# Output product of the linear attention layer as three products of split parts, with x2 held one group at a time

## The reference

```
x = _layernorm(x)                                   # of the outer step
h = _layernorm(x, ln1_g, ln1_b)
Q = phi(h @ Wq); K = phi(h @ Wk); V = h @ Wv        # 16 heads of 64, phi = elu + 1
num_t = Q_t @ sum_{s<=t} K_s V_s^T;  den_t = Q_t . sum_{s<=t} K_s
x = x + (num / max(den, 1e-6)) @ Wo                 # the product that is changed
x = x + gelu(_layernorm(x, ln2_g, ln2_b) @ Wf1) @ Wf2
```

## Time and profile before

| | |
|---|---|
| median of three runs | 4540.95 us |
| the three runs | 4534.86, 4540.95, 4541.82 us |
| the profiled execution, its own time | 4534.58 us |
| its span | 4532.8 us |
| TensorE busy | 4069.8 us, 90% |
| VectorE busy | 2799.5 us, 62% |
| ScalarE busy | 1909.9 us, 42% |
| GpSimd busy | 1185.3 us, 26% |
| HBM traffic | 38 GB/s over the span |
| mean granted TensorE clock | 0.95 |

### The profile page before, as it was taken

How to read it: one execution, slowest core, us unless ns; L and a number is a source line. 1 busy time by engine, 2 the same in 40 slices (tenths; PEclk the granted TensorE clock), 3 DMA queues, 4 the chain that set the end, 5 groups by cost and what they waited for, 6 DMA issues and landing times. The chain is left out here.

```text
span 4532.8 us, 78162 instructions
## 1 busy us (share of the span) xinstructions
PE 4069.8 (90%) x26868; PEld 3109.3 (69%) x26868; DVE 2799.5 (62%) x8170; ACT 1909.9 (42%) x3047; POOL 1185.3 (26%) x1096
## 2 busy tenths in 40 slices
PE   4999999999994899999999999999999599999992
PEld 2344444444442688888888888888888498989892
DVE  4787887887871655565656655555665465555555
ACT  1566665666663333332333433333433233333333
POOL 3233343433422311111111111111111133333334
PEclk8899999999996999999999999999999699999996
DMA  3443443453321100000000000000000133333335
GB/s 70 87 91 62 81 98 54 76 113 59 57 67 58 36 14 16 20 19 11 18 15 16 14 12 16 16 4 14 14 13 27 41 64 61 64 62 64 60 74 205
DMA packets 169072, 222.84 MB, mean 49 GB/s; under 512 B 27148, under 2 KB 144235, under 8 KB 168672
## 3 DMA queue, kind: packets, MB, share of 16 engines
q1 hardware_dynamic: 140640, 181.14, 17.1%
q0 software_dynamic: 25728, 28.03, 4.0%
q10 hardware_dynamic: 2304, 8.39, 0.5%
HBM read 85.92 MB, written 87.05 MB: 38 GB/s over the span
## 5 line engine op out<-in xcount | busy, mean ns | idle before, releaser
L812 ACT ACTIVATE probs<-a_scores 128x1024 f32<-128x1024 f32 (+3 forms) x768 | 614.8, 811 | 367.4 <-PE a_scores L716 361.6
L973 DVE CUSTOM_DVE_ANT_0 a_scores<-a_scores,mask 128x384 f32<-128x384 f32 (+3 forms) x1024 | 482.1, 515 | 117.8 <-PE a_scores L702 112.1
L716 PEld LDWEIGHTS a_scores<-q_st,k_st 50*128 50x128 f32 x1536 | 149.6, 192 | 405.7 <-issue 273.4
L269 POOL TENSOR_TENSOR l_ln_rstd<-l_ln_ve,minus_half 128x4 f32<-128x4 f32 x80 | 84.0, 1050 | 1196.9 <-DVE l_ln_ve L242 1196.7
L716 PE MATMUL a_scores<-q_st,k_st 50*128 50x512 f32 (+3 forms) x1536 | 350.9, 455 | 32.7 <-issue 24.8
L976 DVE TENSOR_REDUCE mx<-a_scores 128x2 f32<-128x1024 f32 x256 | 310.5, 1223 | 109.5 <-PE a_scores L702 108.3
L702 PE MATMUL a_scores<-k_st,q_st 48*128 48x512 f32 (+3 forms) x1536 | 307.1, 398 | 47.6 <-ACT probs L812 29.9
L736 PE MATMUL a_out<-probs,v_aug 128*32 128x512 f32 (+3 forms) x3072 | 347.7, 526 | 1.9 <-POOL probs L905 1.8
L905 POOL TENSOR_SCALAR_AFFINE_SELECT probs<-probs 128x512 f32<-128x512 f32 x256 | 162.7, 636 | 558.7 <-ACT probs L812 555.3
L2333 PE MATMUL e_out<-e_weights_lo,e_hT_hi 128*128 128x256 f32 x1088 | 308.1, 283 | 0.0
L2333 PE MATMUL e_out<-e_weights_hi,e_hT_lo 128*128 128x256 f32 x1088 | 307.6, 283 | 0.0
(11 more groups left out here) (259 smaller groups left out, 10195.4 us busy)
## 6 DMA issues: line engine op xcount, KB each, us to landing
q_st<-parts SPq DMA_DIRECT2D x192, 128.0 KB, 4.4
k_st<-parts SPq DMA_DIRECT2D x192, 128.0 KB, 6.0
expert_rows_scratch<-empty_row SPq DMA_DIRECT2D x34, 520.0 KB, 8.7
e_weights<-in_L_ffn_W_dram SPq DMA_DIRECT2D x16, 1024.0 KB, 6.8
e_rows<-expert_rows_scratch SPq DMA_DIRECT2D x24, 390.0 KB
e_rows<-expert_rows_scratch SPq DMA_DIRECT2D x16, 520.0 KB
x_in<-in_L_attn_x_dram SPq DMA_DIRECT2D x8, 1024.0 KB, 5.7
expert_sums_scratch<-empty_row SPq DMA_DIRECT2D x8, 1024.0 KB, 12.0
```

Of the source, the lines that this page charges most:

```text
L716: last = nc.tensor.matmul(psum_r[:, R.slot(u), h2, 0:w], k_st[rows, 2 * hg + pair, i * P:(i + 1) * P], q_st[rows, 2 * hg + pair, q0:q0 + w ...
L812: nc.scalar.activation(probs[:, k % 3, 2 * pair:2 * pair + 2, 0:w], psum_r[:, R.slot(u), :, 0:w], ACT.Exp).then_inc(R.evacuated[R.slot(u)], 1)
L973: last = nc.vector.tensor_tensor_reduce(s, s, mask[:, HALF - w:HALF], 1.0, LEAST, ALU.add, ALU.max, out[:, h2, :])
```

## The change

The output product becomes three products of split parts (`attention_out`): high by high, high by low, low by high, 96 matmuls in place of 32. `wo` is kept as `hi` and `lo`, split once at the start on VectorE and GpSimd beside Wf1 and Wf2. `oT` has two parts: ScalarE's copy rounds the unit to `hi` in the place of `kT`, and no longer frees the slot; VectorE subtracts `hi` from the PSUM unit into `lo` (`low_outputs`), in the place of `qT`, and frees it. VectorE does so for units 0 and 1 behind chunk 6, 2 and 3 behind chunk 10, 4 and 5 behind chunk 14, 6 and 7 behind chunk 15. `x2` holds one group; SyncE loads group g+1 for the norms, and then group g once more for the residual. `nT2` moves onto the second half of the kept scores.

```diff
-        wo = sb("l_wo", [P, ME, D])
+        wo = {"hi": sb("l_wo_hi", [P, ME, D], F32R)}
+        wo["lo"], raw_o = sb_with("l_wo_lo", [P, ME, D], "l_wo_raw", [P, ME, D])
-        x2 = sb("l_x2", [P, 2, G4, D])
+        x2 = sb("l_x2", [P, G4, D])
-        oT = kT
+        oT = {"hi": hT["lo"], "lo": hT["hi"]}
...
+                def load_again(g, normed):
+
+                    sp.wait_ge(a3_ready, normed)
+                    sp.sem_inc(x2_read, 1)
+                    sp.dma_start(x2[:, :, :], of_group(x2v, g)).then_inc(x2_loaded[1], 16)
...
-                    if not last:
-                        sp.wait_ge(xf_ready, g)
-                        sp.sem_inc(x2_read, 1)
-                        sp.wait_ge(x3_stored, g * 16)
-                        sp.dma_start(x2[:, 1 - s, :, :], of_group(x2v, g + 1)).then_inc(x2_loaded[1 - s], 16)
+                    sp.wait_ge(xf_ready, g)
+                    sp.sem_inc(x2_read, 1)
+                    sp.wait_ge(x3_stored, g * 16)
+                    if last:
+                        sp.dma_start(x2[:, :, :], of_group(x2v, g)).then_inc(x2_loaded[1], 16)
+                    else:
+                        sp.dma_start(x2[:, :, :], of_group(x2v, g + 1)).then_inc(x2_loaded[0], 16)
+                        load_again(g, g + 2)
...
-                def two_tiles(g, u, i, lhs, rhs, nk):
+                def attention_out(g, u, i):
...
-                        for k in range(nk):
+                        terms = [(m, a, b) for m in range(ME)
+                                 for a, b in (("hi", "hi"), ("hi", "lo"), ("lo", "hi"))]
+                        for k, (m, a, b) in enumerate(terms):
                             last = nc.tensor.matmul(psum_g[:, G.slot(u), jj * D:(jj + 1) * D],
-                                                    lhs[:, k, j * P:(j + 1) * P], rhs[:, k, :],
-                                                    start=(k == 0), stop=(k == nk - 1))
+                                                    oT[a][:, m, j * P:(j + 1) * P], wo[b][:, m, :],
+                                                    start=(k == 0), stop=(k == len(terms) - 1))
...
+                    if first:
+                        pe.wait_ge(f_weights, 6)
...
-                        nc.scalar.copy(oT[:, 4 * half:4 * half + 4, j * P:(j + 1) * P],
+                        nc.scalar.copy(oT["hi"][:, 4 * half:4 * half + 4, j * P:(j + 1) * P],
                                        psum_g[:, G.slot(u), :].rearrange("p (m q) -> p m q", m=4)
-                                       ).then_inc(G.evacuated[G.slot(u)], 1)
+                                       ).then_inc(o_hi_ready, 1)
...
+                    pool.wait_ge(x2_loaded[1], g * 16 + 16)
+                    pool.sem_inc(x2_read, 1)
                     pool.wait_ge(a3_normed, g + 1)
...
+                def low_outputs(g, U, units):
+                    for i in units:
+                        u, j, half = U["O"] + i, i // 2, i % 2
+                        dve.wait_ge(o_hi_ready, g * 8 + i + 1)
+                        at = (slice(None), slice(4 * half, 4 * half + 4), slice(j * P, (j + 1) * P))
+                        nc.vector.tensor_tensor(oT["lo"][at],
+                                                psum_g[:, G.slot(u), :].rearrange("p (m q) -> p m q", m=4),
+                                                oT["hi"][at].bitcast(F32),
+                                                ALU.subtract).then_inc(G.evacuated[G.slot(u)], 1)
...
+                        if g4 == 2 and j > 0:
+                            low_outputs(g, U, range(2 * j - 2, 2 * j))
+                    low_outputs(g, U, range(6, 8))
                     if not last_group:
                         high(g, g + 1, U)
```

More of the change, by code:

```diff
@@ L1226, in linear_layer @@
         state = sb("l_state", [P, NP, 2 * DV])
-        scores = sb("l_scores_kept", [P, 2, 2, 4, P])
+        with nc.sbuf_tensor("l_scores_kept", [P, 2, 2, 4, P], F32) as scores:
+            pass
+        sb("l_scores_place", [P, 2, 4, P])
+        nT2_hi, nT2 = sb_with("l_nT2_hi", [P, CD, HALF], "l_nT2", [P, CD, HALF])
         den = sb("l_den", [P, 2, 4])
         o = sb("l_o", [P, 2, E1])
-        oT = kT
+        assert MF == ME
+        oT = {"hi": hT["lo"], "lo": hT["hi"]}
         flat_k = kt[:, :, :].rearrange("p j (a n) -> p (j a) n", n=HALF)
@@ L1309, in linear_layer @@
         xf_ready = sem("l_xf_ready")
+        o_hi_ready = sem("l_oT_hi_ready")
         rows_ready = sem("l_rows_ready")
@@ L1378, in _, with store @@
                                          allow_slow_non_contiguous=True).then_inc(raw_loaded[0], 16)
-                for dst, w in ((wo[:, :, :], Wo), (raw_f[0], Wf1), (raw_f[1], Wf2), (wg[:, :, :], Wg)):
+                for dst, w in ((raw_o[:, :, :], Wo), (raw_f[0], Wf1), (raw_f[1], Wf2), (wg[:, :, :], Wg)):
                     sp.dma_start(dst, w.rearrange("(c p) n -> p c n", p=P)).then_inc(load, 16)
-                def store(g, s):
+                def store(g):
                     sp.wait_ge(x3_ready, g + 1)
-                    sp.dma_start(of_group(x3v, g), x2[:, s, :, :]).then_inc(x3_stored, 16)
+                    sp.dma_start(of_group(x3v, g), x2[:, :, :]).then_inc(x3_stored, 16)
+                def load_again(g, normed):
+                    sp.wait_ge(a3_ready, normed)
+                    sp.sem_inc(x2_read, 1)
+                    sp.dma_start(x2[:, :, :], of_group(x2v, g)).then_inc(x2_loaded[1], 16)
                 def group(g, b, s, U, first, last):
                     if first:
-                        sp.dma_start(x2[:, 1, :, :], of_group(x2v, 1)).then_inc(x2_loaded[1], 16)
+                        sp.wait_ge(a3_ready, 1)
+                        sp.dma_start(x2[:, :, :], of_group(x2v, 1)).then_inc(x2_loaded[0], 16)
+                        load_again(0, 2)
                         return
-                    store(g - 1, 1 - s)
+                    store(g - 1)
                     if last:
@@ L1395, in group @@
                         load_weights(sp, W1, W2, 0, raw_e, e_loaded)
-                    if not last:
-                        sp.wait_ge(xf_ready, g)
-                        sp.sem_inc(x2_read, 1)
-                        sp.wait_ge(x3_stored, g * 16)
-                        sp.dma_start(x2[:, 1 - s, :, :], of_group(x2v, g + 1)).then_inc(x2_loaded[1 - s], 16)
+                    sp.wait_ge(xf_ready, g)
[6 more added lines that the diff above has]
+                        load_again(g, g + 2)
                 groups(sp, group)
-                store(NGR - 1, 1)
+                store(NGR - 1)
                 sp.wait_ge(x3_stored, NGR * 16)
@@ L1818, in _ @@
                 low_weights(2)
-                for n, w in enumerate((wf1, wf2)):
-                    pool.wait_ge(f_weights, 2)
-                    nc.gpsimd.tensor_tensor(w["lo"][:, :, :], raw_f[n], w["hi"][:, :, :].bitcast(F32),
+                for raw_w, w in ((raw_f[0], wf1), (raw_f[1], wf2), (raw_o[:, :, :], wo)):
+                    pool.wait_ge(f_weights, 3)
+                    nc.gpsimd.tensor_tensor(w["lo"][:, :, :], raw_w, w["hi"][:, :, :].bitcast(F32),
                                             ALU.subtract).then_inc(f_weights, 1)
@@ L1846, in first_norms @@
                         dve.wait_ge(a3_ready, g + 1)
-                    src = a3 if call else x2
-                    piece(ln1, dve, g, call, chain1, lambda j: src[:, s, j, :], k)
+                    src = a3[:, s, :, :] if call else x2
+                    piece(ln1, dve, g, call, chain1, lambda j: src[:, j, :], k)
                 def last_norms(g, s, part):
                     call, k = part // 4, part % 4
-                    src = x2 if call else a3
+                    src = x2 if call else a3[:, s, :, :]
                     if part == 0:
@@ L1863, in last_norms @@
                     for j in range(G4):
-                        last = ln3.apply(j, norm[:, j, :] if call else a3[:, s, j, :], src[:, s, j, :])
+                        last = ln3.apply(j, norm[:, j, :] if call else a3[:, s, j, :], src[:, j, :])
                     last.then_inc(xf_ready if call else a3_normed, 1)
@@ L2112, in _ @@
                 dve.wait_ge(load, 64)
-                for n, w in enumerate((wf1, wf2)):
-                    nc.vector.tensor_copy(w["hi"][:, :, :], raw_f[n]).then_inc(f_weights, 1)
+                for raw_w, w in ((raw_f[0], wf1), (raw_f[1], wf2), (raw_o[:, :, :], wo)):
+                    nc.vector.tensor_copy(w["hi"][:, :, :], raw_w).then_inc(f_weights, 1)
                 groups(dve, group)
```

17 lines of the change are left out of this document (7 added, 10 removed).

## The result

The changed kernel took 4557.52 us, the median of 6 runs (4542.73 to 4567.76), and the kernel before 4538.09 us, the median of 6 on the same chip (4530.96 to 4542.47). The ratio is 1.0047, with a 95% interval of 1.0034 to 1.0060: 0.5% slower. The forecast was 4568 us, slower, with a range of 4537 to 4592.

The account below looks back on a forecast made before the run. TensorE's work and waits in the linear layer were taken as the bound: 4534.58 - 33.3 (product) + 49.1 (waits) + 13.6 (clock) = 4564 us, plus 3.8 for the middle of the runs: 4568 us, range 4537 to 4592.

Parts of the forecast that it names:

- What bounds the kernel: Linear layer: TensorE is busy 9 tenths, so a microsecond off its work, or of its waiting, is worth a microsecond.
- The gain: Output product: 96 split matmuls take 11.62 us for 13.70, 2.08 us less per group, 33.3 us in 16 groups.
- The four-pass rule: Output product: FP32 takes four passes, so three give 10.3 us; as a rival 4533 or 4546 us, chance 0.05.
- The waits: Eight subtractions on VectorE make TensorE wait at chunks 6, 10, 14 and 15: 3.07 us per group, 49.1 us in all.
- The end's 0.66: Behind chunk 15: the last subtraction ends near 2483.35, and the product that started at 2482.74 waits for it, +0.66 us.
- VectorE's wait behind chunk 9: VectorE's idle 0.73 us there is a wait for TensorE, late by the same 1.29 us, so it gives nothing back.
- The price of a subtraction: On VectorE: 1.29 us per pair, by the mask row; lower end 0.43 us and upper 0.69 us each.
- The net of +0.99 us per group: Linear layer: waits of 3.07 us less the product's gain of 2.08 us; over 16 groups +15.8 us.
- The clock: Chunk 9's wait grows from 0.82 to 2.11 us; clock falls in every second group, 8 x 1.7 = +13.6 us.
- The rest: Splitting the output weights once at the start, and the single x2 buffer with its second load: no time.
- no clock falls: Rival, chance 0.25: the waits are as computed, but 2.1 us is not enough to lower TensorE's clock; 4550 to 4555 us.
- faster: Rival, chance 0.12: subtractions cheaper or better hidden, especially behind chunk 6; 4529 to 4535 us, or 4512 to 4518 with room there.

Follow-up runs that it names:

- the product alone: The change without subtractions, the 96 split matmuls kept and the high part of `o` read in place of the low: 4497.38 us against 4528.35, ratio 0.9937.
- The two kernels run again: The unedited change and the kernel before, each timed and profiled once more: 4556.42 us (ratio 1.0052) and 4529.98 us (ratio 0.9992).
- the subtractions alone: The change with its eight subtractions, but one f32 product of the high parts: 4592.28 us against 4532.43 for the kernel before, ratio 1.0134.
- x2 alone: The change's single x2 buffer, loaded twice, and moved `nT2`, with the kernel before's f32 product and single copies: 4531.87 us against 4528.35, ratio 1.0006.
- chunk 14's pair early: The change with only chunk 14's pair of subtractions moved to that chunk's head, ahead of its numerator: 4531.98 us against 4530.98, ratio 1.0000.
- the order alone: The change with next rows turned ahead of the last tile's `o`, and only the product's second half awaiting the last subtraction: 4520.98 us against 4532.43, ratio 0.9978.

## Why the prediction was right

**What bounds the kernel.** Right. In the linear layer each microsecond on TensorE or of its waits arrives in the time; the kernels with one part each show it from both sides (2.30 us per group off, 3.27 us on).

**The gain.** 11.58 us in the trace for 11.62 forecast, and 2.30 us per group by the run with the product alone, for 2.08. The other 0.2 us lie in the matmul behind the product, which no term of the forecast had. Behind the f32 product it took 0.58 us and the next started 0.42 us after it (2496.44 to 2496.86); behind the split product it takes 0.39 us and the next starts after 0.23 us (2513.78 to 2514.01). The four-pass rule of the Trainium skill ("FP8 and Floating Point Precision", section TensorE Precision Notes) gives an estimate of 10.3 us, three single passes for four. The trace does not agree with that: the 96 matmuls follow each other every 0.12 us and take 11.58 us.

**The waits.** 3.07 us were forecast and 3.28 measured. The two kernels run again have the steadier groups: in the eighth the product starts 55.81 us behind the group's first score with the change and 52.53 us before, and the run with the subtractions alone has 3.27. (In the two first profiles it is 56.14 and 53.22, 2.92 us, for that group of the kernel before was a long one.) By places: the update of chunk 9 comes 1.08 us later, for 1.29 forecast; the pair of chunk 10 adds 0.48, for 0.16; that of chunk 14 adds 0.89, for 0.96; the end adds 0.83, for 0.66. So the first term was too large and the second and the last too small, and the sum was nearer than its parts. The end's 0.66 was also not what the forecast's own two times give, which is 0.61 (2482.74 to 2483.35). VectorE's wait behind chunk 9 gave nothing back, as said: it is 0.31 us in both of the kernels run again, and 0.73 and 0.69 in the first profiles. The price of a subtraction, taken from the mask's pair, was right within 0.1 us, since what follows a pair starts 1.20 us after it. The net of +0.99 us per group measured 0.94 to 0.99. That this is so close is partly luck, since gain and waits were both forecast 0.2 us too small.

**The clock.** The step held in kind and was too large. The wait at chunk 9 is 1.63 us (1.47 in the first group, and 0.49 in the last, which has no norms of a next group), not 2.11. The state sum comes 1.08 us later and not 1.29, and TensorE has already lost 0.21 us at chunk 8, so that it comes to chunk 9 later by that. The forecast named the wait at chunk 8, but did not take it off. Behind some of these waits the clock falls, as expected. TensorE's timeline and the view by windows of the changed kernel (PEclk is the third value from the end):

```profile
2349.93 0.96 PE L1624 MATMUL l_update<-l_v,l_k 128*128 128x130 f32 x4 [1.63 <-DVE l_state L2095]
2350.68 1.70 PE L1503 MATMUL l_general<-ident,l_o 128*128 128x128 f32 x7
```

```profile
2350.20:2353.60 3.40, 3.40 (x22) 3.07 (x23) 1.92 (x11) 1.17 (x2) 2.32 (x3) 0.51 0.03 9
2353.60:2357.00 3.40, 3.40 (x36) 3.28 (x34) 2.44 (x7) 2.08 (x4) 2.05 (x4) 0.99 0.10 34
```

For 3.4 us TensorE runs at 1.2 GHz and then at 2.4 again. In a group with such a stretch the product starts 1.4 to 1.7 us later, near the price of 1.7. But over the two profiles of the change it follows the chunk-9 wait in 8 of the 30 groups that have it (all but the last), where I took one in two. In the first profile three more stretches stand elsewhere in the groups, so that there were six there, and five in the second. At some 1.6 us each that is 8 to 10 us for the 13.6 forecast, and the kernel before has some as well, with no such waits: one in the first profile, three in the second. So 2 to 5 of them more stand in the change's profiles, 3 to 8 us.

**The rest.** At nothing, as forecast: x2 alone gives 1.0006. From the layer's first turned rows to the first score it is 50.57 us in the change run again and 50.56 in the kernel before run again, so the split of `wo` costs nothing either. The third cast starts at 1511.00, takes 1.21 us, and the next phi at 1513.88 still waits 1.66 us for ScalarE.

**Sum.** 16 groups at 0.94 to 0.99 us are 15 to 16 us, the clock adds 3 to 8: 18 to 24 us, and 19 and 24 us were measured. From the first group's first score to the last's the change takes 18.2 us longer than the kernel before, both run again (1940.01 and 1921.85), and 19.3 in the first profiles. The forecast's sum was 29.4, and what it had too much is the clock term; the measured time lies 10 us under it. Of the rivals, "no clock falls" (4550 to 4555 us) came nearer to the measured time than the forecast did, though the clock did fall; "faster" needed room behind chunk 6, which there is not. It can be had elsewhere: the pairs stood behind the state sum, when ahead of the numerator VectorE is waiting for TensorE in any case.

## What to carry to other kernels

When an engine off the bound is given work, the sum of its busy time says little; find the instruction behind which the bounding engine waits and put the new work just after a place where the loaded engine itself was waiting. The same eight subtractions cost 3.3 us per group behind the state sums, and about 1 us once six of them stood ahead of the numerators and the first half of the product no longer waited for the last. But moving work within a stretch that has no gaps mostly moves the waits. Where runs differ by less than half a per cent, compare the time of one repeated stage in the traces: here a group was good to 0.2 us in all profiles but one, where whole runs of one kernel scattered by 10 to 37.

## What was not expected of the hardware

The granted clock fell behind the wait at chunk 9 (1.47 to 1.63 us) in 8 of the 30 groups of the change that have this wait and stayed at full in the others, with the same instructions around it each time. Five kernels' profiles have the wait at this length: the change twice, the subtractions alone, chunk 14's pair early and the order alone. Together they show the fall in 18 of 75 groups. In the eight others, where no wait for the state sum is over 1.1 us, there is none behind chunk 9 in 128 groups. So the longer wait brings the falls, but not each time. Nor is it the only place: when the kernel before was run again, three stretches stood elsewhere in its groups; in the kernel with x2 alone, whose waits are the same, there were none. What decides in which groups the clock falls stays open.
